# Reciprocals of the softmax denominators, taken once for each query between two 32x32 block transposes on the vector engine

## What is computed

```python
xf = x.reshape(b, din, hw)
Q = einsum('kc,bcp->bkp', q_w, xf)
K = einsum('kc,bcp->bkp', k_w, xf)
V = einsum('vc,bcp->bvp', v_w, xf)
S = einsum('bkp,bkq->bpq', Q, K)
A = softmax(S, axis=-1)
z = einsum('bpq,bvq->bvp', A, V)
```

## Time and profile before

| what | us |
|---|---|
| median of 3 runs | 2080.59 |
| lowest and highest | 2080.13, 2082.37 |
| the profiled execution's own time | 2084.49 |
| its span, first to last instruction | 2082.7 |
| mean granted PE clock in it | 0.924 of full |
| DVE busy in it | 1596.4 |
| POOL busy in it | 1341.5 |

### The profile page before, as it was taken

The page is one execution under the profiler, slowest core; times in us unless marked ns, Lnnn a source line. Parts: engine busy times, 40 slices in busy tenths (PEclk is TensorE's granted clock), DMA queues, the critical chain, the costliest instruction groups (busy, mean ns, idle before and its releaser), DMA issues.

```text
span 2082.7 us, 30055 instructions
## 1 busy us (share of the span) xinstructions
PE 1869.7 (90%) x7932; PEld 696.8 (33%) x7932; DVE 1596.4 (77%) x2642; ACT 865.8 (42%) x1064; POOL 1341.5 (64%) x702
## 2 busy tenths in 40 slices
PE   5877999999878799999987789999998779999996
PEld 4352222223336122222333622222233442222221
DVE  5747888887874788888786478888879557888883
ACT  2132554546314145454622324545461333454553
POOL 3510788989650179898954037989886205798887
PEclk9986999999888699999988869999999887999998
DMA  1003000000000300000000210000000030000000
GB/s 76 0 0 78 1 6 5 5 8 7 6 1 12 66 1 6 10 5 4 5 6 1 37 41 6 5 5 5 4 5 5 0 47 0 6 5 5 4 4 9
DMA packets 8505, 26.08 MB, mean 13 GB/s; under 512 B 2256, under 2 KB 5840, under 8 KB 7888
## 3 DMA queue, kind: packets, MB, share of 16 engines
q1 hardware_dynamic: 8400, 24.79, 5.1%
HBM read 8.73 MB, written 6.42 MB: 7 GB/s over the span
## 4 chain that ended last, share of the span: by engine, by line
PE 63%; issue 13%; DVE 10%; POOL 9%; ACT 2%; SPq 1%; DMA 1%; POOLq 1%; DVEq 0%; ACTq 0%
PE PS L1165 27%; PE PS L1112 14%; PE PS L1097 11%; DVE nmt L617 3%; DVE nmt L610 2%; POOL accP L943 2%; DVE accD L694 2%; POOL VT L905 1%; PE PS L1083 1%; POOL VT L900 1%; POOL VT L902 1%; PE PS L1070 1%; PE PS L1061 1%; POOL VT L909 1%; PE PS L1122 1%
## 5 line engine op out<-in xcount | busy, mean ns | idle before, releaser
L826 ACT ACTIVATE Pb<-PS 128x896 f32<-128x896 f32 (+1 forms) x700 | 640.5, 917 | 629.2 <-PE PS L1112 611.4
L943 POOL TENSOR_TENSOR accP<-accP,Pb 128x896 f32<-128x896 f32 x364 | 832.3, 2287 | 46.3 <-ACT Pb L826 20.5
L610 DVE TENSOR_REDUCE nmt<-PS 128x1 f32<-128x448 f32 x1176 | 663.6, 613 | 164.1 <-PE PS L1097 163.2
L1165 PE MATMUL PS<-Pb,VT 128*64 128x448 f32 x2800 | 693.5, 573 | 11.9 <-ACT Pb L826 9.3
L1112 PE MATMUL PS<-Qa,Ka 99*128 (+3 forms) x1400 | 478.3, 363 | 1.0 <-ACT Qa L810 1.0
L1097 PE MATMUL PS<-Ka,Qa 96*128 96x448 bf16 x1176 | 394.4, 356 | 24.3 <-DVE nmt L610 23.4
L694 DVE TENSOR_TENSOR accD<-accD,Pb 128x896 f32<-128x896 f32 x168 | 301.8, 1796 | 42.2 <-ACT Pb L826 40.6
L1112 PEld LDWEIGHTS PS<-Qa,Ka 99*128 99x128 bf16 (+1 forms) x1400 | 125.1, 98 | 540.5 <-issue 490.2
L936 POOL TENSOR_TENSOR accQ<-Pb 128x896 f32<-128x896 f32 x28 | 61.7, 2203 | 267.2 <-ACT Pb L826 267.2
L1165 PEld LDWEIGHTS PS<-Pb,VT 128*64 128x64 f32 x2800 | 145.7, 136 | 239.0 <-issue 193.5
L526 DVE SCALAR_TENSOR_TENSOR Pb<-PS,cf,xnp 128x448 f32<-128x448 f32 x252 | 154.8, 675 | 12.6 <-PE PS L1020 8.8
(11 more groups left out here) (138 smaller groups left out, 1488.4 us busy)
## 6 DMA issues: line engine op xcount, KB each, us to landing
xin<-in_x SPq DMA_DIRECT2D x4, 1568.0 KB, 6.6
out<-xw SPq DMA_DIRECT2D x28, 224.0 KB, 1.9
Qa<-parts SPq DMA_DIRECT2D x48, 98.0 KB, 4.0
Ka<-parts SPq DMA_DIRECT2D x48, 98.0 KB, 4.1
wz<-in_weights SPq DMA_DIRECT2D x1, 829.0 KB, 7.9
cs<-in_cst SPq DMA_DIRECT2D x1, 576.0 KB, 8.5
wz<-in_weights SPq DMA_DIRECT2D x1, 576.0 KB, 9.4
cs<-in_cst SPq DMA_DIRECT2D x1, 256.0 KB, 6.3
```

What stands on the lines that cost most here:

```text
L610: nc.vector.reduce_max(nmt[:, i // NJ, i % NJ:i % NJ + 1], PS[0:BLK, bank, 0:CH], X, negate=True).then_inc(mx_free, 1)
L826: nc.scalar.activation(Pb[0:r, j % PSLOTS, :, :], PS[0:r, b:b + 2, 0:CH], ACT.Exp).then_inc(exp_done, 1)
L943: nc.gpsimd.tensor_tensor((accQ if j < TO_ACCP else accP)[:, :, :], (accQ if j <= TO_ACCP else accP)[:, :, :], Pb[:, j % PSLOTS, :, :], AL ...
L1165: last = mm(PS[C * h:C * h + C, OB, 0:CH], VT[:, j, C * h:C * h + C], Pb[:, j % PSLOTS, h, :], start=(j == 0), stop=(j == NQ - 1))
```

## The change

The four quarters become one sequence in step 3. The 448 denominators are transposed out of bank 7 in blocks of 32 x 32 into `Rr`. Since the 32 rows of a block are equal, each row of the transposed block holds the denominator of one query in all 32 columns; one column of each of the 14 blocks goes into the reciprocal, 14 columns in all, into `Rc`. A second transpose reads each of these columns 32 times and writes `Rr` as it was before. DVE waits for itself twice, by a new semaphore `rstep`. The two waits ahead (`d_ready`, `fin_done`) stay, and so does the signal `recip` behind the last instruction. Steps 4 to 6 have no part in it any more.

```diff
-QUART = CH // 4
+SQ = 32
...
+        Rc = sb("Rc", [P, CH // SQ])
...
+        rstep = sem("reciprocal_step")
...
-                def reciprocals(sidx, i):
-
-                    if i == 0:
-                        dve.wait_ge(d_ready, sidx + 2)
-                        dve.wait_ge(fin_done, sidx + 1)
-                    ins = nc.vector.reciprocal(Rr[:, i * QUART:(i + 1) * QUART], PS[:, 7, i * QUART:(i + 1) * QUART])
-                    if i == 3:
-                        ins.then_inc(recip, 1)
+                def reciprocals(sidx):
+
+                    dve.wait_ge(d_ready, sidx + 2)
+                    dve.wait_ge(fin_done, sidx + 1)
+                    nc.vector.transpose(Rr[:, :], PS[:, 7, 0:CH]).then_inc(rstep, 1)
+                    dve.wait_ge(rstep, 2 * sidx + 1)
+                    nc.vector.reciprocal(Rc[:, :], Rr[:, 0:CH:SQ]).then_inc(rstep, 1)
+                    dve.wait_ge(rstep, 2 * sidx + 2)
+                    nc.vector.transpose(Rr[:, :].rearrange("p (a b) -> p a b", b=SQ),
+                                        Rc[:, :].unsqueeze(2).to_broadcast([P, CH // SQ, SQ])).then_inc(recip, 1)
...
-                        if FINISH_STEP <= j < FINISH_STEP + 4 and not first:
-                            reciprocals(sidx - 1, j - FINISH_STEP)
+                        if j == FINISH_STEP and not first:
+                            reciprocals(sidx - 1)
...
-                for i in range(4):
-                    reciprocals(NJ * g + NJ - 1, i)
+                reciprocals(NJ * g + NJ - 1)
```

## The result

The kernel after takes 2114.06 us (median of 4 runs, 2110.83 to 2118.08), the kernel before beside it 2081.48 us (4 runs, 2080.13 to 2082.70): ratio 1.0155, 95% interval 1.0142 to 1.0167, so 32.6 us slower.

What follows compares the result with a forecast made beforehand. PE sets the pace in the attention stage. Stalls of +32.6 us and group ends of -0.9 give +31.7 on the profiled 2084.49, so 2116.2; that execution was 3.9 above the median, hence 2112 us, range 2099 to 2124.

Steps and rivals of the forecast that it cites:

- The copy loses its place: Step 3, 20 superblocks: copy waits for POOL's sum; PE stalls 1.54 us (even) or 1.69 us (odd), +32.6 us.
- Any sequence between 0.8 and 2.8 us puts the copy behind the same POOL sum: Step 3: within these limits the stall term hardly depends on how long the transposes take.
- faster: Step 3: new instructions under 0.80 us together keep the copy ahead of POOL; 2072 us, chance 0.04.
- The sequence: Step 3: transposes 0.61 us each, reciprocal 0.24, self-waits 0.06 each; 1.58 us, about 1.5 until the next instruction starts.
- T2 takes the same turn: Step 3: second transpose also waits for POOL's sum, the copy for one more; 2160 us, chance 0.08.
- Superblock 6, nothing: Last superblock of each group, which has no tiles at step 5: no change in time taken.
- Group ends, -0.9: Third group's end and kernel's end gain 1.4 us each; two ends with a backward jump lose 0.97 each.

Runs made afterwards that it cites:

- the spread kernel: Kernel after with first transpose, reciprocal and second transpose one to a step (steps 3, 4, 5), all three together only at group ends: 2079.54 us, ratio 0.9990.

## Why the prediction was right

Predicted 2112 us (+31.7 on the profiled execution's time), measured 2114.06 (+32.6 between medians, +26.3 between the spans of the two profiles). The mechanism, the copy's lost place, carried the forecast and came as described. That the total fits within 2 us is in part luck: two smaller terms missed by 1.6 us together, and more than that was made up outside the edited code. By its steps:

- **The copy loses its place, 1.54 and 1.69 in 20 superblocks, +32.6.** Measured 1.54 and 1.69 to 1.70, 32.7 in all. The 0.41 from POOL's end to the maximum, read off superblock 0, held in every line shown. That it is the place and no other cause is shown by the four kernels with a wider first quarter and by the copy moved ahead.
- **"Any sequence between 0.8 and 2.8 us puts the copy behind the same POOL sum."** Right in kind: one transpose more changes no superblock, three more cost the next sum. The lower limit was mis-sized. It took the hold for beginning at POOL's recorded start, 0.80 us after the first reciprocal's. The copy still goes first when recorded 0.06 behind, and no longer at 0.15: from the first reciprocal's start to the copy's that is 0.86 and 0.96 us, and the limit lies between them. The forecast didn't depend on it, as the sequence takes 1.52 (311.57 to 313.09; 1.50 predicted); the point at which the rival *faster* turns did.
- **The sequence.** T1 and T2 0.64 and 0.65 for 0.61, R 0.24 for 0.24, and the gap at a self-wait 0.03 to 0.04 (312.25 less 311.57 + 0.64) for 0.06. The two errors cancel. Where transposes follow one another without a wait, three of them take 1.62 from start to start (315.59 to 317.21), so one takes 0.54 of the engine's time, and the record's 0.64 overlaps its neighbour. The Trainium skill's figures give 0.54 by the prediction's estimate ("Vector Engine (DVE) Microarchitecture Reference", section 5.2), and the trace agrees.
- **T2 takes the same turn.** This rival didn't come true: T2 keeps 0.65 with POOL busy. Of the two statements of the Trainium skill that I set against each other, that of "Vector Engine (DVE) Microarchitecture Reference", section 5.1, fits this trace. One pattern was tried, a source read with a step of zero.
- **Superblock 6, nothing.** In the three groups that another follows, from its first exponential to the end of the last denominators it takes 0.4 less (58.0 to 57.6). DVE's last sum ends 0.5 later. But PE has been idle for only 0.78 us when the denominators begin, and runs the eight in 1.7 us at a granted clock of 1.00; before it had been idle for 2.23, and took 2.7 at 0.61. The prediction had no term for that clock. The miss is 1.3 us together. The first four, after and then before:

```profile
1592.63 0.98 PE L1125 MATMUL PS<-accP,ones 128*64 128x448 f32 x4 [0.78 <-DVE accD L698]
```

```profile
1571.05 1.21 PE L1122 MATMUL PS<-accP,ones 128*64 128x448 f32 x4 [2.23 <-DVE accD L694]
```

and the windows of all eight, after and then before:

```profile
1592.60:1594.40 1.80, 1.77 (x9) 0.62 (x10) 0.00 (x0) 1.77 (x3) 0.00 (x0) 1.00 0.00 0
```

```profile
1571.05:1573.80 2.75, 2.75 (x9) 0.72 (x10) 0.00 (x0) 0.51 (x2) 0.00 (x0) 0.61 0.00 0
```

- **Group ends, -0.9.** Measured +0.69 and +0.88 at the looped ends (predicted +0.97 each) and -1.36 and -1.38 at the others (-1.4 each): -1.2. The cause given, a jump reached later because of the self-waits, fits: with the old quarters there, the 0.7 to 0.9 are gone.

What was left out are the stages between a group's first tap and its first exponential, in which nothing is edited. They take 651.2 us in all four groups in the profile of before and 647.4 in that of after, 647 to 654 in the others, without an order that I could find; the cause stays open. That is the remainder of the profiled difference: spans differ by 26.3, which is 32.7 - 1.3 - 1.2 - 3.8, less 0.1 in superblock 0. Between medians the difference is 32.6, 2.4 more than the 30.2 of the edited stages. These stages may also be why the runs of one kernel spread over some 5 us, but each kernel has only one trace, so this isn't shown.

## What to carry to other kernels

Before an instruction is made longer or moved, look at the one behind it, and at what the other engine starts within some tenths of a microsecond of that: here a VectorE copy of 896 columns between SBUF buffers and a GpSimd sum exclude each other for a whole instruction, so 0.1 us of delay cost PE 1.5. Spread a new sequence over the slots that the old one had; if it must stand in one piece, put it behind the instruction that has a turn to lose. And DVE time saved where PE sets the pace buys nothing but this margin.

## What the runs showed of the hardware

- The hold of a GpSimd sum doesn't begin at its recorded start: a copy recorded 0.06 us later still went first (POOL's record then grows from 2.08 to 2.56), copies recorded 0.14 and 0.15 later did not. The Trainium skill ("Perfetto Trace Analysis", section "GPSIMD Engine Instruction") says that the recorded start is where one of the engine's processors asks for its tensor; by that rule a hold taken a little later is plausible, but no run here shows what happens in between.
- A loser waits for the whole instruction: started 0.15, 0.36, 0.51, 0.71 and 1.24 us behind POOL, the copy takes 2.40, 2.20, 2.06, 1.85 and 1.32 us and always ends 0.47 to 0.49 behind POOL's end. A reduction of the same 896 columns (1.04 us), transposes (T2 0.65) and reciprocals (R 0.23 at 310.58 in the spread kernel) aren't held beside a busy POOL.
- A PE stall of 3.5 us in a stage at full clock is followed by 3.8 us at a granted clock of 0.55; a stall of 1.4 us is not (1.00). At the end of superblock 6, 2.23 us of idle time are followed by a granted clock of 0.61 in the denominators, and 0.78 us by 1.00.
- A backward jump in DVE's program costs 2.5 us of idle time behind a chain of three short instructions that wait for each other, and 0.3 behind 3 us of independent work. Where no jump follows, the tap comes without idle time.
